# Two cross-attention layers over a 1601-row context: the weighted sums gathered in every third step of a hand-written unit order

## The reference, cut to what matters

```python
q, k, v = heads(norm(x) @ Wq.T), heads(ctx @ Wk.T), heads(ctx @ Wv.T)   # 16 heads of 16
attn = softmax(einsum('bhqd,bhkd->bhqk', q, k) / 4, axis=-1)
x = x + merge(einsum('bhqk,bhkd->bhqd', attn, v)) @ Wo.T
# layer 0 then: a small attention over heads, and a mixture of experts with one pick
# layer 1 then: a linear scan over the rows, GELU and a norm, and a routed FFN (3 matrices, 8 experts, top 2)
```

## Time and profile before

| | before |
|---|---|
| median of 3 runs | 1015.02 us (1014.58 to 1016.22) |
| span of the profiled execution | 1012.9 us |
| PE busy | 945.4 us, 93% of the span |
| DVE busy | 612.7 us, 60% |
| ACT busy | 554.5 us, 55% |
| mean granted TensorE clock | 0.987 |

### The profile page before, as it was taken

One profiled execution on the slowest core, in us unless ns is written; L12 is line 12 of the kernel. 1 busy time (PEld: TensorE's weight loads), 2 busy tenths in 40 slices (PEclk: granted clock), 3 DMA queues, 4 the chain that ended last, 5 costly groups with the idle time before them and its releaser, 6 DMA issues.

```text
span 1012.9 us, 35591 instructions
## 1 busy us (share of the span) xinstructions
PE 945.4 (93%) x15476; PEld 624.4 (62%) x15476; DVE 612.7 (60%) x1022; ACT 554.5 (55%) x1056; POOL 198.6 (20%) x233
## 2 busy tenths in 40 slices
PE   5589889999999999999999999998899999999998
PEld 2256555656666665666666666666678544445887
DVE  6456656577476656758666786785774774435322
ACT  5368676677767767665666656756634622212200
POOL 4212112121211112121121221213446200000000
PEclk9789999999999999999999999999799999999999
DMA  8677484553635443444344345324211432232100
GB/s 303 192 225 224 114 260 125 160 167 90 194 89 155 129 109 89 120 116 127 88 132 137 94 118 137 83 54 152 85 57 33 163 125 83 83 125 83 43 1 22
DMA packets 70829, 123.79 MB, mean 122 GB/s; under 512 B 34770, under 2 KB 46082, under 8 KB 67412
## 3 DMA queue, kind: packets, MB, share of 16 engines
q1 hardware_dynamic: 69812, 119.84, 39.8%
q0 software_dynamic: 576, 1.35, 0.4%
q10 hardware_dynamic: 288, 0.33, 0.1%
HBM read 64.81 MB, written 17.32 MB: 81 GB/s over the span
## 4 chain that ended last, share of the span: by engine, by line
PE 74%; DVE 10%; ACT 7%; issue 4%; SPq 3%; POOL 2%; DMA 1%; ACTq 0%; POOLq 0%; DVEq 0%
PE ps L717 72%; DVE mpart L1366 3%; ACT p L1122 3%; SPq L472 3%; DVE rinv L1383 2%; PE ps L856 1%; DVE cl L1341 1%; POOL xg L658 1%; ACT ch L1080 1%; PE ps L886 1%; DMA qbscratch<-qb 1%; ACT k L1096 1%; ACT kh L1097 1%; DVE oT L1386 1%; ACT L1122 0%
## 5 line engine op out<-in xcount | busy, mean ns | idle before, releaser
L1366 DVE TENSOR_REDUCE mpart<-ps 128x2 f32<-128x800 f32 (+1 forms) x256 | 252.3, 988 | 140.8 <-PE ps L717 139.6
L1122 ACT ACTIVATE p<-ps 128x512 f32<-128x512 f32 (+1 forms) x416 | 225.4, 595 | 175.2 <-PE ps L717 173.9
L646 POOL TENSOR_TENSOR kl<-k,kh 128x400 f16<-128x400 f32 (+1 forms) x128 | 118.2, 925 | 450.0 <-ACT kh L1097 450.0
L717 PE MATMUL ps<-p,v 128*17 128x64 f32 x6656 | 133.1, 223 | 2.1 <-issue 2.1
L717 PEld LDWEIGHTS ps<-p,v 128*17 128x17 f32 x6656 | 98.9, 98 | 39.4 <-issue 37.4
L717 PE MATMUL ps<-wvh,ch 128*128 128x256 f16 (+1 forms) x416 | 115.1, 277 | 0.0
L717 PE MATMUL ps<-wvl,ch 128*128 128x256 f16 (+1 forms) x416 | 114.2, 275 | 0.0
L717 PE MATMUL ps<-wvh,cl 128*128 128x256 f16 (+1 forms) x416 | 114.2, 274 | 0.0
L717 PE MATMUL ps<-xcl,wh 128*128 128x512 f16 (+2 forms) x384 | 112.9, 308 | 0.0
L717 PE MATMUL ps<-xch,wh 128*128 128x512 f16 (+2 forms) x384 | 112.8, 308 | 0.0
L717 PE MATMUL ps<-xch,wl 128*128 128x512 f16 (+2 forms) x384 | 112.8, 308 | 0.0
(11 more groups left out here) (208 smaller groups left out, 1447.8 us busy)
## 6 DMA issues: line engine op xcount, KB each, us to landing
ks<-kh SPq DMA_DIRECT2D x256, 100.1 KB
w<-in_wgu SPq DMA_DIRECT2D x16, 1024.0 KB, 4.8
ks<-kl SPq DMA_DIRECT2D x128, 100.1 KB
w<-in_wd SPq DMA_DIRECT2D x8, 1024.0 KB, 4.8
c32a<-in_ctxT SPq DMA_DIRECT2D x16, 400.5 KB, 4.7
cparts<-ch SPq DMA_DIRECT2D x8, 800.5 KB, 6.2
cparts<-cl SPq DMA_DIRECT2D x8, 800.5 KB, 8.6
c32a<-in_ctxT SPq DMA_DIRECT2D x12, 400.0 KB, 3.2
```

The source lines that it names most:

```text
L646: nc.gpsimd.tensor_tensor(kl[:, mt, k0:k0 + w], k32[:, ku % 2, 0:w], kh[:, mt, k0:k0 + w], ALU.subtract).then_inc(sem("klo_done"), 1)
L717: return nc.tensor.matmul(o, lhsT, rhs, start=start, stop=stop, skip_group_check=shared)
L1122: nc.scalar.activation(p32[0:n, step % PRING, BANK * side:BANK * side + BANK], ps[0:n, side, :], ACT.Exp, scale=DH ** -0.5).then_inc(sem(" ...
L1366: nc.vector.reduce_max(mpart[:, j0:j0 + 3:2, quarter], o.rearrange("p (b c) -> p b c", b=2)[:, :, 0:w], AX.X).then_inc(sem("max_done"), 1)
```

## The change

The table is written anew. Every step begins with S and a P unit. The weighted sums of three key tiles stand together in steps 3, 6, 9 and 12 (`WEIGH_AT`), and the one of the last key tile in step 0 of the next round. The other steps hold K, N and V units. `E` marks where the next position of the token events stands: thirteen per round as before, but two each in steps 2, 5, 7 and 10, one in steps 0, 1, 8, 11 and 12, and none in steps 3, 4, 6 and 9. ACT walks the table as written. O stands ahead of V6 and K4 in step 4, both halves of the division come before the maximum of P6, and two of the four context pieces are one step later. The instructions are the same ones in another order. The core of the diff, with two lines of the table of either side:

```diff
-STEP_UNITS = {0: ["V2", "S", "P0", "W"],
...
-              4: ["K4", "S", "P5", "W", "O"],
...
-WEIGH_AT = {0: (11,), 1: (12,), 3: (0, 1), **{k: (k - 2,) for k in range(4, KT)}}
-SUMS_STEP, DIVIDE_STEP = 2, 5
-
-SECOND_BANK = ("V3", "V5", "K4", "K5", "K7", "V1", "N1", "N3")
+STEP_UNITS = {0: ["S", "P0", "W", "P1", "V2", "E"],
...
+              4: ["S", "P5", "O", "V6", "K4"],
...
+WEIGH_AT = {0: (12,), **{k: (k - 3, k - 2, k - 1) for k in (3, 6, 9, 12)}}
+SUMS_AFTER, DIVIDE_AFTER = "P2", "K4"
+
+SECOND_BANK = ("V3", "V5", "K4", "K6", "V0", "N0", "N2")
...
-CTX_STEPS = {3: 0, 5: 1, 7: 2, 9: 3}
+CTX_STEPS = {3: 0, 6: 1, 8: 2, 9: 3}
...
-def scores_first(units):
-
-    at = units.index("S")
-    if at and units[at - 1][0] in "KNV":
-        return units[:at - 1] + ["S", units[at - 1]] + units[at + 1:]
-    return units
+def slots_of(k):
+
+    before = sum(STEP_UNITS[i].count("E") for i in range(k))
+    return iter(range(before, before + STEP_UNITS[k].count("E")))
...
+                        elif name == "E":
+                            for what, layer, t in events(g, next(slots)):
+                                event(what, layer, t)
...
-                        if k == SUMS_STEP and name == "P2" and g:
+                        if name == SUMS_AFTER and g:
                             take_sums(g - 1)
-                    if k == DIVIDE_STEP and g:
-                        divide(g - 1, 1)
+                        if name == DIVIDE_AFTER and g:
+                            divide(g - 1, 1)
```

More of the change, by code:

```diff
@@ L57 @@
 FIRST_CTX_LOW = {"P4": 4, "P6": 5, "P8": 6, "P10": 7}
-STEP_UNITS = {0: ["V2", "S", "P0", "W"],
-              1: ["V3", "S", "P1", "W"],
-              2: ["V4", "P2", "V5", "S", "P3"],
-              3: ["W", "S", "P4"],
-              4: ["K4", "S", "P5", "W", "O"],
[L63 to L70, removed]
-WEIGH_AT = {0: (11,), 1: (12,), 3: (0, 1), **{k: (k - 2,) for k in range(4, KT)}}
-SUMS_STEP, DIVIDE_STEP = 2, 5
-SECOND_BANK = ("V3", "V5", "K4", "K5", "K7", "V1", "N1", "N3")
+STEP_UNITS = {0: ["S", "P0", "W", "P1", "V2", "E"],
+              1: ["S", "P2", "V3", "E"],
+              2: ["S", "P3", "E", "V4", "V5", "E"],
+              3: ["S", "P4", "W"],
+              4: ["S", "P5", "O", "V6", "K4"],
+              5: ["S", "P6", "E", "K5", "E"],
+              6: ["S", "P7", "W"],
+              7: ["S", "P8", "E", "K6", "K7", "E"],
+              8: ["S", "P9", "V0", "P10", "V1", "E"],
+              9: ["S", "P11", "W"],
+              10: ["S", "P12", "E", "N0", "P13", "N1", "E"],
+              11: ["S", "P14", "N2", "E"],
+              12: ["S", "P15", "W", "T", "N3", "E"]}
+WEIGH_AT = {0: (12,), **{k: (k - 3, k - 2, k - 1) for k in (3, 6, 9, 12)}}
+SUMS_AFTER, DIVIDE_AFTER = "P2", "K4"
+SECOND_BANK = ("V3", "V5", "K4", "K6", "V0", "N0", "N2")
 OWN_UNITS = ("V2", "V3", "V4", "V5", "V6")
-CTX_STEPS = {3: 0, 5: 1, 7: 2, 9: 3}
+CTX_STEPS = {3: 0, 6: 1, 8: 2, 9: 3}
 PRING = 4
@@ L176, in has_unit @@
 def has_unit(name, g):
-    return name in ("S", "W") or 0 <= round_of(name, g) < G
+    return name in ("S", "W", "E") or 0 <= round_of(name, g) < G
 def turn_index(name, layer, t):
@@ L232, in users_before @@
         for k in range(KT):
+            slots = slots_of(k)
             for name in STEP_UNITS[k]:
+                if name == "E":
+                    for event in events(g, next(slots)):
+                        if event_read_by(*event):
+                            before[event] = last[3]
+                            last[3] = event_read_by(*event)
+                    continue
                 if name in ("S", "W") or not has_unit(name, g):
@@ L238, in users_before @@
                 last[at] = read_by(name, r)
[L239 to L242, removed]
     before["O", G - 1] = last[3]
@@ L601, in _ @@
                         store_parts(g + 2)
[L602 to L607, removed]
+                    for slot_ in slots_of(k):
+                        for name, layer, t in events(g, slot_):
+                            event(name, layer, t)
+                            if name == "stage" and t + 2 < STAGE_JOBS:
+                                load_stage(t + 2)
+                            elif name == "stage" and t == STAGE_JOBS - 1:
+                                store_expert_bias()
                     if (g, k) == (2, 0):
@@ L701, in _ @@
                             klo(round_of(name, g), int(name[1]))
-                    for name, layer, t in events(g, k):
-                        event(name, layer, t)
+                        elif name == "E":
+                            for what, layer, t in events(g, next(slots)):
+                                event(what, layer, t)
             for item in TAIL:
@@ L978, in _ @@
                             scores(g, k)
-                        elif name == "W" and k > 1:
+                        elif name == "W" and k:
                             for kt in WEIGH_AT[k]:
@@ L984, in _ @@
                                 weigh(g - 1, kt)
+                        elif name == "E":
+                            for what, layer, t in events(g, next(slots)):
+                                event(what, layer, t)
                         else:
                             run_unit(name, round_of(name, g))
[L987 to L991, removed]
+            for kt in WEIGH_AT[0]:
+                weigh(G - 1, kt)
             parts, last_parts = iter(GATE_PARTS), iter(LAST_GATE_PARTS)
@@ L1256, in _ @@
                 for k in range(KT):
-                    for name in scores_first(STEP_UNITS[k]):
+                    slots = slots_of(k)
+                    for name in STEP_UNITS[k]:
                         if name == "S":
                             exps(g, k)
+                        elif name == "E":
+                            for what, layer, t in events(g, next(slots)):
+                                event(what, layer, t)
                         elif name != "W" and has_unit(name, g):
@@ L1598, in _ @@
                 for k in range(KT):
+                    slots = slots_of(k)
                     for name in STEP_UNITS[k]:
-                        if name not in ("S", "W") and has_unit(name, g):
+                        if name == "E":
+                            for what, layer, t in events(g, next(slots)):
+                                event(what, layer, t)
+                        elif name not in ("S", "W") and has_unit(name, g):
                             after_unit(name, round_of(name, g))
-                        if k == SUMS_STEP and name == "P2" and g:
+                        if name == SUMS_AFTER and g:
                             take_sums(g - 1)
-                    if k == DIVIDE_STEP and g:
-                        divide(g - 1, 1)
+                        if name == DIVIDE_AFTER and g:
+                            divide(g - 1, 1)
                     if k in CTX_STEPS and g + 2 < B:
                         split_ctx(4 * (g + 2) + CTX_STEPS[k])
-                    for name, layer, t in events(g, k):
-                        event(name, layer, t)
             take_sums(G - 1)
```

## The result

The changed kernel takes 1040.41 us (median of 4 runs, 1035.69 to 1040.85), the kernel before 1015.59 in the same session (4 runs, 1014.58 to 1016.22). The ratio is 1.0236, with a 95% interval of 1.0214 to 1.0258: slower by 24.8 us, where 13.6 were forecast on the span.

The account below looks back on a forecast made before the run. The prediction took PE's queue, busy for 93% of the span, as the bound. Switches saved 16.7 us and new waits outweighed them: +13.6 on 1012.9 gives 1026.5, forecast as a 1029 us median, range 1014 to 1045.

Parts of the forecast that it names:

- Switches: PE's order: 167 fewer changes between kinds of matmul, 0.10 us each, save 16.7 us.
- P1: Step 0: only W between P0 and P1, so PE waits 0.59 in 14 rounds, 1.17 in round 0; 9.4 us.
- P7: Both division halves now precede P6's maximum on DVE, so P7 waits longer, S6 too in layer 0; 6.6 us.
- T and S0: Round's end: T waits 0.13 for the maxima (2.0 us), next S0 0.22 for row copies (1.8 us); together 3.8 us.
- Context: Rounds 0 to 5: context splits delay S10, P12 and P13, 2.1 a round against 1.2 of old waits; 5.5 us.
- Events: Token events' DVE work between close maxima: some ten places at 0.5 us each, 5 us.
- The last round: No P, K or N units; ACT paces S at least 1.65 apart in either order; counted as nothing, with 4 either way.
- the part on the switch: PE's queue: 756 switches become 589, worth 16.7 us (13 to 22), called the whole gain as no instruction is removed.
- the signs named: Profile after: waits about 0.6 behind a lone W, 0.7 to 1.0 before P7, maxima well over 20, PE busy some 15 less.
- DVE keeps up: Rival: faster, maxima late only at P1, T and S0; 1011.5 us, or 1000 without old waits; chance 0.27.
- The clock falls earlier: Rival: round 15's clock falls some 10 us earlier, doubling 6 us of work; 1035 us; chance 0.08, within slower.
- PSUM Bottleneck: Skill page: packing doesn't speed emptying of PSUM; read as holding where P units stand close, not everywhere.

Follow-up runs that it names:

- e1_single: The changed kernel with one key tile's W in each of steps 4 to 12 again (step 3 keeps three): 1083.59 us, ratio 1.0689 to the kernel before.
- e2_p1: The changed kernel with P1 moved to step 1, P2 to step 2, P3 between V4 and V5: 1031.21 us, ratio 1.0155 to the kernel before.
- e5_pairs: The kernel before with W of two tiles in every second step, three in step 1: 1025.12 us, ratio 1.0088 to the kernel before.
- b2_three: The kernel before without W in steps 6, 8 and 10, two tiles in 7, 9 and 11: 1019.19 us, ratio 1.0035 to the kernel before.
- the three repairs: The changed kernel with P1 in step 1, step 0's event behind W, the division's second half behind P6's maximum: 1023.07 us, ratio 1.0092 to the kernel before.
- The padding: The changed kernel with 64 small matmuls more at PE's start, before its first transpose: 1062.61 us, ratio 1.048 to the kernel before.

## Why the prediction was right, and where its sum was not

Slower was right, and 1040 lies inside the range, 11 us above the forecast. By its steps:

- **Switches, -16.7.** PE's busy time fell by 9.0 only. But PE was busy for 32.0 us at half clock, and for 18.8 before, and half of such time is the clock's, an estimate. Without it the fall is 15.6, for 167 switches. The same estimate gives 6.8, 15.8, 11.3 and 5.5 in the runs e1_single, e2_p1, e5_pairs and b2_three, for 69, 151, 96 and 49: a switch is worth 0.09 to 0.12 in all five, and the gain is right. Three tiles of W with their exit take 1.46, as worked out: in round 0 of the changed kernel

```profile
72.91 1.53 PE L721 MATMUL ps<-p,v 128*17 128x64 f32 x96
74.37 0.41 PE L721 MATMUL ps<-qcur,ks 64*128 64x64 f16 x16
```

- **P1, 9.4.** Right: 7.9 by the waits, 8 to 9 by the run that moved it. (Before, an event, V3 and S stood between P0 and P1 beside W; V2, named with V3 in the part on the change, stood ahead of P0.)
- **P7, 6.6.** The sum is near, the place half of it. P7 waits 3.3 in rounds 1 to 5; S6 waits in rounds 1 to 14, 6.1 in all, and from round 6 on it alone; the old waits at P7, all gone, were 4.4. That leaves 5.0. That ACT's chain is as long as DVE's there was seen only as a side remark; with DVE alone repaired, S6 waited as before.
- **T and S0, 3.8.** T's half did not come: PE waits for m 3.3 us in all, 3.5 before. S0's came: 2.1 where 1.8 was forecast, listed under "issue", as shown above.
- **Context, 5.5.** Wrong: P12 and S10, with P13 in round 1, wait some 4.6 in rounds 1 to 5, but the waits at P11 and on the lo parts that went were 5.1, so the term is about nothing. The new waits, 2.1 a round in the sum, are 0.9: 0.55 at P12 and 0.45 at S10 in place of 0.7 each, and P13's hardly came. About 2 a round is what the old steps cost in the new order, for which it was not worked out.
- **Events, 5.0.** Too small. P3, the transposes behind it, and P10, P12 and P14 beside events wait some 10 us, and S4 another 3.4 in rounds 11 to 14. In round 0 an event's weight split (`fwh` on ACT, `fwl` on DVE) puts 1.80 before P10 and 0.90 before S12. In rounds 11 and 13 the rows of ACT show a table load of 1.28 behind a gate's activation, ahead of the exponentials of step 3, which only W covers (the kernel before has the same load behind that activation, and no S waits there):

```profile
569.10 1.28 ACT L1127 ACT_TABLE_LOAD   x1
```

- **The last round, 0.** Right: from its S0 to the end it is 322.2 us before and 322.8 now.
- **Not in the sum at all:** 10.0 us of waits for instructions (12.1, and 2.1 before), and the half clock of rounds 0, 1, 8 and 10, some 6.6. The step that failed is the end of the part on the switch, "That is the whole gain: no instruction is removed". No instruction is removed, but three tiles of them are read in 1.46, and the sum took that for free. That the density is what makes them late agrees with the runs and is not shown by itself. The view behind the earlier trace rows has a second line, issue with 2.1 us in 3 times, two of them about 1 us long at p,v matmuls; the prediction passed over it.

The terms for waits were summed to 30.3 and PE's idle time rose by 34.8; that they are close is partly chance, since terms too large made room for one that was missing. What the sum missed on the span, 12.2 us, is 7.7 of busy time, of which the clock is some 6.6, and 4.5 of idle. Of the signs named, a wait at P1 came (0.52, about 0.6 was named), and one at P7 in five rounds (0.63 to 0.71, 0.7 to 1.0 was named); the maxima stayed just short of 20 us (19.0 between 60 and 540), and the busy time fell by too little.

Of the rivals, "DVE keeps up" fell at the point it gave: P7 with S6 alone is worth more than 3.5 us. "The clock falls earlier" was right that fits and starts bring the clock down, and wrong on the place: round 15 kept its 10.2 us, and rounds 0, 1, 8 and 10 fell. The page TensorEngine Tiling (Array Packing) of the Trainium skill, "PSUM Bottleneck", held as it was read, at places: P units 1.43 apart are set by the maximum, while DVE is busy for 59%; and the exponentials, which empty PSUM on ACT, came to cost nearly as much.

What stays open: when a packet of instructions is asked for, and so what sets such a wait. That each ends behind a packet is shown. Denser W brings more of them (1.1, 2.1 and 2.8 us with W in nearly every step, 5.4 and 8.5 with pairs, 12.6 in the change, always between 60 and 540), but orders with the same three tiles range from 5.6 to 14.6, and how far one kernel's executions differ is not known, as each has one trace. At the ends the sum is small where PE waits more for maxima: 31.5 and 6.5 with the context pieces in the old steps, 9.2 and 14.6 with the three repairs. In between it is not: 17.3 and 7.7 with the division moved, 19.0 and 12.6 in the change. So whether a wait that is repaired is taken up by the next supply stays open. That a busy q1 makes them longer is only suggested by the window at 101 us; it wasn't tried, since the restacking can't be taken away without a race.

## What to carry to other kernels

Before short instructions are gathered to spare switches, count them by the time they take: a stretch that reads instructions faster than the rest is a stretch in which their supply can end last, and the profile shows that only as "issue". Look first whether such a wait ends just behind something that it reads, as S0's does. A unit that looks like plain work may be the cover of three waits (P, S and T here), so work out for each step which result is late when the unit leaves. Two waits of one us close together, or one of over two, can cost more than their sum, as the matmuls behind them may run at half clock; taking the pair apart gave 4 to 7 us here.

## What was not expected of the hardware

- PE stands for up to 2.8 us within one group of 32 like matmuls (3.2 in the run with pairs), each time until 2.3 to 2.8 us after a 16 KB packet of q8 began.
- The granted clock falls to a half in the middle of a busy kernel: behind waits of 1.15 and 0.99 close together the V units ran at 0.22 a matmul in place of 0.11, in seven of twelve such places; and in rounds 0 and 1 it fell 1.5 and 1.4 us behind the end of a wait for instructions of 2.38 and 2.78.
- The padding's 64 matmuls of 16 columns in f32 are recorded as 128, each with a weight load, and took 27.3 us, 0.21 for each record. The trace has no granted clock for that stretch, so its level is not known.
